# Mixing matmuls of an attention kernel: one weight tile of 92 columns becomes two, of 64 and 28 columns

## What is computed

```python
dots = jnp.einsum('bhid,bhjd->bhij', q, k) * scale
attn = jax.nn.softmax(dots, axis=-1)
attn = jnp.einsum('bhij,hg->bgij', attn, reattn_w)     # the mixing
a = attn.transpose(0, 2, 3, 1)                         # layer norm over the 8 heads
mu = jnp.mean(a, axis=-1, keepdims=True)
var = jnp.mean((a - mu) ** 2, axis=-1, keepdims=True)
a = (a - mu) * jax.lax.rsqrt(var + LN_EPS) * ln_g + ln_b
attn = a.transpose(0, 3, 1, 2)
out = jnp.einsum('bhij,bhjd->bhid', attn, v)
```

## Time and profile before

| | |
|---|---|
| median of three runs | 714.72 us (713.38 to 714.96) |
| the profiled execution's own time | 717.34 us |
| its span, first to last instruction | 715.5 us |
| TensorE (PE) matmul busy | 646.5 us, 90% of the span |
| TensorE weight loads (PEld) busy | 578.4 us, 81% |
| VectorE (DVE) | 506.8 us, 71% |
| ScalarE (ACT) | 415.8 us, 58% |
| GpSimd (POOL) | 406.2 us, 57% |
| mean granted TensorE clock | 0.964 of full |

### The profile page before, as it was taken

The page is one execution under the profiler, slowest core; times in us unless marked ns, Lnnn a source line. Parts: engine busy times, 40 slices in busy tenths (PEclk is TensorE's granted clock), DMA queues, the critical chain, the costliest instruction groups (busy, mean ns, idle before and its releaser), DMA issues.

```text
span 715.5 us, 18159 instructions
## 1 busy us (share of the span) xinstructions
PE 646.5 (90%) x5880; PEld 578.4 (81%) x5880; DVE 506.8 (71%) x1543; ACT 415.8 (58%) x1382; POOL 406.2 (57%) x495
## 2 busy tenths in 40 slices
PE   4687979999999999999999999999999999986666
PEld 3576869888898889888888988898888888875565
DVE  2845576868777877878687778878787877765532
ACT  2265557565675757575656757575656657563312
POOL 1534446657493847656574938476565848374603
PEclk9799889999999999999999999999999999999877
DMA  6000020030202020110202020201202020302020
GB/s 206 1 23 1 23 86 23 13 104 1 95 21 95 21 95 21 67 50 1 98 18 95 21 95 21 95 21 45 71 1 95 21 97 1 97 2 96 0 90 17
DMA packets 16634, 36.69 MB, mean 51 GB/s; under 512 B 1440, under 2 KB 13664, under 8 KB 14560
## 3 DMA queue, kind: packets, MB, share of 16 engines
q1 hardware_dynamic: 16608, 36.35, 16.0%
HBM read 33.14 MB, written 3.20 MB: 51 GB/s over the span
## 4 chain that ended last, share of the span: by engine, by line
PE 64%; DVE 21%; issue 5%; POOL 5%; ACT 2%; DMA 2%; POOLq 0%; SPq 0%; DVEq 0%; ACTq 0%
PE ps_fill L394 13%; PE ps_mix L599 11%; PE ps_fill L395 11%; PE ps_fill L396 11%; PE ps_dots L588 7%; DVE xn L941 6%; PE ps_av L607 5%; PE ps_fill L543 5%; POOL rstd L1179 2%; DVE stats L927 2%; DVE key L970 2%; DVE aT L1022 2%; DVE hot L973 1%; DMA spread<-weights 1%; DVE mv L932 1%
## 5 line engine op out<-in xcount | busy, mean ns | idle before, releaser
L466 POOL TENSOR_TENSOR act_split_lo<-act,act_split_hi 128x736 fp32r<-128x736 f32 (+1 forms) x80 | 128.2, 1606 | 33.3 <-ACT act_split_hi L805 33.3
L1147 POOL TENSOR_TENSOR sum<-sq 92x384 f32<-92x384 f32 x64 | 64.5, 1007 | 117.5 <-ACT sq L747 117.5
L739 ACT ACTIVATE ex<-ps_dots,negmax 128x92 f32<-128x92 f32 x384 | 123.4, 333 | 13.3 <-DVE negmax L1003 13.3
L599 PE MATMUL ps_mix<-mixk,probs 128*92 128x128 f32 x768 | 101.9, 285 | 16.3 <-DVE aT L1024 16.0
L599 PEld LDWEIGHTS ps_mix<-mixk,probs 128*92 128x92 f32 x768 | 89.6, 166 | 25.0 <-issue 17.5
L1100 DVE SCALAR_TENSOR_TENSOR act<-ps_fill,b_neg,spread 128x368 f32<-128x368 f32 x128 | 72.9, 591 | 49.5 <-PE ps_fill L396 42.3
L1141 POOL TENSOR_TENSOR probs<-ex,rinv 128x552 f32<-128x552 f32 x64 | 71.2, 1113 | 30.0 <-DVE rinv L1009 30.0
L588 PE MATMUL ps_dots<-xT,yT 128*64 128x92 f32 x1536 | 74.9, 247 | 7.6 <-ACT ex L739 3.9
L747 ACT ACTIVATE sq<-ps_mix 92x768 f32<-92x768 f32 x64 | 51.4, 804 | 48.1 <-PE ps_mix L599 48.0
L588 PEld LDWEIGHTS ps_dots<-xT,yT 128*64 128x64 f32 x1536 | 63.4, 137 | 18.3 <-issue 11.3
L739 ACT ACTIVATION_READ_ACCUMULATOR ex<-ps_dots,negmax 128x1 f32 x384 | 78.1, 203 | 0.0
(11 more groups left out here) (160 smaller groups left out, 1697.9 us busy)
## 6 DMA issues: line engine op xcount, KB each, us to landing
spread<-weights SPq DMA_DIRECT2D x16, 1472.0 KB, 6.2
xin<-in_x SPq DMA_DIRECT2D x16, 320.0 KB
out<-ostage SPq DMA_DIRECT2D x16, 160.0 KB
act<-w_raw SPq DMA_DIRECT2D x2, 576.0 KB, 7.3
xin<-in_x SPq DMA_DIRECT2D x16, 52.0 KB
qkv<-qk_raw SPq DMA_DIRECT2D x1, 512.0 KB, 5.3
out<-ostage SPq DMA_DIRECT2D x16, 24.0 KB
spread<-tok_raw SPq DMA_DIRECT2D x1, 256.0 KB, 3.6
```

Source lines behind the costliest of these rows:

```text
L466: eng.tensor_tensor(lo, act1[:, two, :], hi.bitcast(F32), ALU.subtract).then_inc(units_ready, 1)
L599: last = pe.matmul(ps_mix[0:N, c // HALF, o:o + 128], probs[:, (s - 1) % 2, c, :], mixk[:, :, :].rearrange("p g i -> p (g i)"), start=True ...
L739: last = act.activation(ex[:, s % 2, c, :], ps_dots[:, c // HALF, o:o + N], ACT.Exp, bias=negmax[:, c:c + 1], accum_out=sums[:, s % 2, c:c ...
L1147: pool.tensor_tensor(sum4[:, :, :, :], sq[:, :, 0:4, :], sq[:, :, 4:8, :], ALU.add)\
```

## The change

The matmul of each chunk in `mix` becomes two: one with weight columns 0 to 63, which writes partitions 0 to 63 of `ps_mix`, and one with weight columns 64 to 91, which writes partitions 64 to 91. Both read the same moving operand. `DH` is 64. Steps, waits and signals keep their places.

```diff
                     for c in range(CHUNKS):
                         o = 128 * (c % HALF)
-                        last = pe.matmul(ps_mix[0:N, c // HALF, o:o + 128], probs[:, (s - 1) % 2, c, :],
-                                         mixk[:, :, :].rearrange("p g i -> p (g i)"), start=True, stop=True)
+                        for first, end in ((0, DH), (DH, N)):
+                            last = pe.matmul(ps_mix[first:end, c // HALF, o:o + 128],
+                                             probs[:, (s - 1) % 2, c, first:end],
+                                             mixk[:, :, :].rearrange("p g i -> p (g i)"), start=True, stop=True)
                     last.then_inc(mix_ready, 1)
```

## The result

The changed kernel takes 890.28 us (median of four runs, 887.07 to 897.04) against 714.58 us (four runs, 713.38 to 714.96): ratio 1.2475, 95% interval 1.2392 to 1.2557. Forecast were 891 us and slower. The profiled execution is the longest of its four: own time 897.04 us, span 895.2 us, 179.7 us more span than before, mean granted clock 0.956.

A forecast was written before the change was run, and what follows sets the result against it. TensorE, busy 90% of the span, was taken to bound the kernel. 717.3 us + 185 for mixes + 1 for edges - 10 for waits gave 893, or 891 on the median's scale; range 718 to 950.

The forecast's parts named there:

- Alternating tiles that pay for each change of width: In `mix`, 64- and 32-column tiles alternate without overlap: 0.70 us per chunk in place of 0.218, 185 us in all; 65%.
- Its parts: Per chunk of `mix`: four records of 0.109 us, two changes at 0.10 each, plus 0.02 and 0.04 for bare weights.
- The edges: Changes of width entering and leaving `mix`: 0.53 us per period in place of 0.48, 1 us more over 16 periods.
- the first rival: In `mix`, narrow and wide tiles overlap, so only edges count: 0.25 to 0.39 us per period more, 720 us; 20%.
- The waits: TensorE's 0.52 us wait before `mix`3 goes as VectorE gains room: about 7 us, plus 3 in first and last periods.
- What was said of `sq` and `av`: Behind `mix`, ScalarE's `sq` comes up to 2.9 us later after its `mix` began, but `av` finds `aT` as now.
- the sum of 893.3: Whole run, profiled execution: 717.3 us plus 185 for mixes plus 1 for edges less 10 for waits, given as 893.
- The clock rival: In every `mix` the clock falls to half, so passes take twice the time: 167 us on top, 1,060 us; 4%.

The follow-up runs named there:

- e1_33: The changed kernel with the second tile taking 33 weight columns in place of 28, the five more being padding: 716.74 us, ratio 1.0036.
- e2_64: The changed kernel with the second tile taking 64 weight columns in place of 28, 36 of them unused: 716.19 us, ratio 1.0041.
- e3_three32: The changed kernel with three tiles of 32, 32 and 28 columns in place of 64 and 28: 718.79 us, ratio 1.0059.
- e4_grouped: The changed kernel with all six matmuls of 64 columns first in each `mix`, then all six of 28: 802.68 us, ratio 1.1245.
- f3: The changed kernel with `av`2 moved from ahead of the routing matmuls to just ahead of `mix`3: 899.10 us, ratio 1.2565.
- g1: The kernel before with the third reciprocal step, `inv`2, and GpSimd's multiplication behind it moved behind the routing's second part: 706.67 us, ratio 0.9908.

## Why the prediction was right, and where it was not

**Alternating tiles that pay for each change of width: right, and shown.** The starts are 0.695 us per chunk where 0.70 was said. e1_33 and e2_64 take the change of width away and the time with it; e3_three32 shows the narrow tile innocent; e4_grouped prices a change at 0.129 us by the records and 0.137 by the medians, forecast 0.13. The Trainium skill, "TensorEngine Tiling (Array Packing)", section Key Properties, says that a change of the tiling mode drains the engine, and a move within it does not. By that rule, if 28 columns are another mode than 33 and 64, e1_33 had to be fast and the change slow. The runs agree: from one tile to the next the starts are 0.20 us apart in the changed kernel, and 0.01 in e1_33. They show the price and what it hangs on; that the array drains meanwhile is the word of the Trainium skill, and no row shows its inside.

**Its parts.** Nothing streams for 0.093 us (0.10 said), and bare weights add 0.02 and 0.05 us (0.02 and 0.04), though not where the profile was forecast to show them: they lengthen the step within a tile (0.13 and 0.16), and the step across is 0.20 both ways. A `mix` came to 2.80 us more and not 2.89: six chunks at 0.695 are 4.17 us and not 4.20, from its start to the next step it is 4.14 on average, and the `mix` of before, averaged in the same way, is 1.34 and not 1.31. 64 x 2.80 = 179 where the sum had 185.

**The edges: counted a little too high.** 0.05 us more per period was said. But `dots` ahead of `mix` takes 0.99 us from start to start now (380.63 to 381.62) where it took 1.10, so the entries from `dots` and `av` save about 0.2 us per period. Against that, `mix`2 is now entered through a change: its first record comes 0.20 us behind the transposes' last one where it came 0.11 (404.41 to 404.61, 323.49 to 323.60), and the products behind `mix`0 and `mix`1 wait 0.02 us more each for their weights. Net 0.07 us per period are saved, 1 us in all. In the first rival the error was larger: it gave 0.25 to 0.39 us per period, and e1_33, which is that rival built, has 39.58 us, 0.04 more.

**The waits: this step failed.** I let the 0.52 us before `mix`3 go, 10 us in all, because VectorE would have 11 us more room per period. It did not go: 0.60 us in the timeline above, 17.0 us in the whole run after 16.0 before. The waits of TensorE over the 13 steady periods, before (108.5 to 622.5 us) and after (130 to 784 us):

```profile
PE ps_mix L599 <- DVE aT L1024: 6.9, 13, 0.6
...
PE ps_fill L543 <- DVE xn L941: 2.2, 13, 0.2
```
```profile
PE ps_mix L600 <- DVE aT L1026: 7.9, 13, 0.7
...
PE ps_dots L588 <- issue: 3.0, 11, 0.4
```

What went are two waits for `xn`, ahead of TX2 and ahead of V3. The list has 2.2 us of the first and none of the second, because the modelled end of the record in front covers them; the starts and the weight loads show them. V2's last matmul and the weight load of V3's first, in the kernel before:

```profile
327.82 0.39 PE L396 MATMUL ps_fill<-wvT_hi,xT_split_lo 128*92 128x512 f32 x1
328.25 0.16 PEld L394 LDWEIGHTS ps_fill<-wvT_hi,xT_split_hi 128*92 128x92 f32 x1 [0.51 <-DVE xn L941]
```

V3 starts 0.43 us behind V2's last matmul there and 0.23 in the changed kernel (411.35 to 411.58), and its own second matmul saves another 0.08; ahead of TX2 0.24 us go. That is 0.52 us per period. A new gap of 0.17 us has come between TX and YF (412.88 to 413.37, where 329.63 to 329.95 was usual).

The reason why the wait for `aT` stayed I read from the traces: it is as long as the chain from RT's product over the routing and `scale` to `aT`, less TensorE's work from RT to `mix`3, and the change put no `mix` between these. The chain is 5.74 us where it was 5.51, and 0.17 of the difference is taken up by the new gap. VectorE's load had nothing to do with it. f3, which was to test this, does not settle it, since it lengthened the chain as well; g1 does, from the other side: the chain 0.55 us shorter, the wait of 0.52 gone. What was said of `sq` and `av` held: ScalarE's `sq` waits 179.2 us for `mix` where it waited 48.0, and over those 13 periods TensorE waits for `aT` ahead of `mix`3 alone, never ahead of an `av`.

**What made up for it.** In the middle stretch 52 x 2.80 = 145.6 us of mixes, less 0.9 for the edges, less 6.8 for `xn` (13 x 0.52), plus 2.2 for the new gap and 1.0 for `aT`, make 141.1; 139.9 were measured. The 1.2 us between, 0.09 per period, I leave open. In the first and last stretch 12 mixes at 2.80 are 33.6 us and 39.8 were measured. The 6.2 us on top go with the clock: it was 0.84 and 0.83 there, where it had been 0.86 and 0.89, and a `mix` at half clock costs more than one at full clock. These 12 mixes together take 61.8 us from their starts to the next steps where they took 20.6, so they alone grew by 41.2. One of them:

```profile
112.50 7.10 PE L600 MATMUL ps_mix<-mixk,probs 128*64 128x128 f32 x24 [3.94 <-DVE aT L1026]
```

Its counterpart before lasts 2.84 us: 4.26 us more in place of 2.8. So the sum of 893.3 for the profiled execution was 5.8 too high for mixes, 1.9 for edges and 1.2 for what is left open, 6.4 too low for waits (10 taken off, 3.6 gone), and had nothing for 6.2 of clock: 897.0, as measured. That execution was 6.8 us above its median, where the prediction took off 2.6. The hit is the mechanism's; that it is so close is partly luck: errors of 6 us stand on both sides. The clock rival (half clock in every `mix`) did not occur: 1.00 from 130 to 784 us.

## What to carry to other kernels

Ask of two matmuls that follow each other whether they use the same width class, not whether their columns are apart: 28 columns beside 64 made a step three times as long; padding the 28 to 33 gave nearly all of it back (ratio 1.0036), and doing all of one width first gave back half. When a wait shall vanish because work was added elsewhere, find its chain and ask whether the work lies on the chain, on the other side of it, or in front of both. By the reasoning above only the second can fill the wait; f3 tried that and gained nothing, because the chain grew by as much. Shortening the chain itself worked. And look at the minimum against the median of small operations on the chain: 0.19 against 1.04 us pointed to the reordering that made this kernel 0.9% faster.

## What was not expected of the hardware

**GpSimd holds VectorE.** A VectorE operation with two inputs of 92 x 32 takes 0.19 us alone, 1.04 us (median of 16 in the kernel before) while GpSimd multiplies into `probs`, and 2.62 us in f3 behind three GpSimd operations, where it ends 0.06 us after them. The Trainium skill, "SBUF — State Buffer", section "SBUF: two separate sides", calls the port pair that these two engines share an exclusive lock for a whole instruction; the runs agree, and show that the loser can wait through several instructions of the other.

**A change of width leaves 0.093 us with nothing streaming also between tiles that share no column**, the same as between full width and 64 (0.09 from the transposes to `mix`2, 0.10 in the earlier trace rows). And records of float32 matmuls on tiles of one width start within 0.02 us of each other, in twos and threes, so that in e3_three32 three of them take little more than the time of one (a `mix` of 1.44 us, where one full-width tile takes 1.34).
